# Where sixteen shared-expert steps stand in a fused transformer kernel: all of them in the routing stage, four before the scores of the second half

## The chip, the cores and the metric

The kernel runs on one core of one Trainium2 chip. The metric is the device time of one execution in microseconds (us), as a median of several runs. The engines are named as the profile names them: PE (TensorE, matrix products), DVE (VectorE), ACT (ScalarE), POOL (GpSimd, which here issues the indirect DMAs) and SP (SyncE, which issues plain DMAs).

## The reference, cut to what matters

A sandwich of four sublayers on x of 8 x 256 tokens by 256 channels: each sublayer is `x = x + layernorm(f(layernorm(x)))` with f = attention, a mixture of experts, a state-space layer and a dense feed-forward. The change touches the mixture alone:

```python
logits = flat @ router_w                                   # 2048 x 64
scores = softmax(logits); topk_idx = top_k(logits + router_bias, 4)
# ... the four scores of a token, made to sum to 1, go into comb (2048 x 64)
g = silu(einsum('nd,edf->nef', flat, wg)); u = einsum('nd,edf->nef', flat, wu)
routed = einsum('ne,nef,efd->nd', comb, g * u, wd)         # 64 experts of 64 hidden
sg = silu(einsum('nd,sdh->nsh', flat, swg)); su = einsum('nd,sdh->nsh', flat, swu)
shared = einsum('nsh,shd->nd', sg * su, swd)               # 2 shared experts of 256 hidden
return routed + shared
```

The shared experts have 512 hidden channels in all, and every token passes through them.

## The kernel before

The 2048 tokens are 16 tiles of 128, in four chunks of 512 (NCH = 4, TPC = 4 tiles each). The program is a row of stages, each one block of five instruction streams (one an engine, run in the order written) with a barrier between blocks. Inside a block the streams are ordered by semaphores alone. The stages that matter here are, in order: routing (`stage_route`, L858 to L1288), the routed experts (`stage_slots`, L1291 to L1456), summing (`stage_mid`, L1467 to L1964, which also starts the state-space layer).

**The routing stage** takes the four chunks one after another.
- PE turns the normed rows of a chunk into columns (`turn`, L971, eight transposes of 128 x 128 a chunk) and multiplies them with the router (`score`, L985, 24 products of 64 columns a chunk). ACT and DVE cut each turned bank into a high and a low part (`high_parts` L1073, `low_parts` L1141), because a 32-bit product is made as three products of parts.
- DVE picks the four experts of each token (`choose`, from L1147), PE counts them (`place_chunk`), DVE makes tables of counts (`tables`) and then, for each chunk, the slot of each token and expert (`find_slots`, L1199 to L1220).
- POOL writes the rows to their slots in DRAM by 64 indirect DMAs (`slots_in<-rows,slots`, L957), 16 a chunk, two in flight; before a chunk's first one it waits for that chunk's `find_slots`.
- SP waits for all 64 and then loads the first of 32 groups of slots (`load_quad`, L851), on which the next stage begins.

**A shared-expert step** is one quarter of the hidden channels (SHARED = 4) for one chunk of tokens, so there are sixteen. In a step PE makes gate and up (12 products of 128 x 512: six into `pg`, six into `pu`, L1032), ACT takes silu of the gate (L1111), DVE multiplies (`prod`, L1236), ACT copies the product's high part (`hh`, L1115), DVE subtracts it for the low part (`hl`, L1240), and PE multiplies down (12 products of 256 columns into `acc`, L1042). `pu` is one bank, so the up part of a step waits for the product of the step before. After four steps ACT takes the sum of a chunk out (`take`, `y<-acc`, L1104). The banks `acc0`, `acc1` and `pg0` are also the banks into which `turn` writes.

Eight steps (chunks 0 and 1) stand at the end of the routing stage: on PE behind `place_chunk(3)`, on DVE the first between `find_slots(2)` and `find_slots(3)`, the others behind it, mixed with the work on the tokens' shares (`moved`, `share`, L1282 to L1285). The other eight (chunks 2 and 3) stand at the start of the summing stage. For them the routed-expert stage loads the shared weights again (four loads of 384 KB), and ACT and DVE split them again.

**The summing stage** starts with POOL, which fetches the four expert outputs of every token (`fetch`, `back<-slots_out,slots`, L1582: four indirect DMAs a tile, 64 in all), into eight buffers. DVE adds them into y (`combine`, L1861), and then the chain of two norms of a chunk runs: DVE's statistics, POOL's power (L1590) and shift (L1593), ACT's normed rows (L452), twice, then PE projects the chunk into the state-space layer. POOL's one queue holds the fetches and the two norms of every chunk. Its order is written out:

```python
for i in range(TPC):
    fetch(i)
...
    first = (2, 2, 2, 0)[g]      # tiles of the next chunk fetched ahead of this chunk's norms
    for i in near[:first]: fetch(i)
    deviations(OF_Y, g)
    for i in near[first:first + 1]: fetch(i)
    deviations(OF_X, g)
    for i in near[first + 1:]: fetch(i)
```

Of the kernel before, what the change touches and what calls it, by code (L numbers as in the profile page):

```python
# [5 lines left out]
F32 = mybir.dt.float32  # L6
# [7 lines left out]
P = 128  # L14
# [796 lines left out]
LATE = 2  # L811
NOW = NCH - LATE
LATE_STEPS = SHARED * LATE
# [44 lines left out]
def stage_route(chip, x, rows, norms, xh, xl, y, ident, xs, t, ahead, router, ins):  # L858
# [7 lines left out]
    STEPS = SHARED * NOW  # L866
    slots, share, owner = t["slots"], t["share"], t["owner"]
    wh, wl, bias, sums, places, sh, sl = (router[n] for n in ("wh", "wl", "bias", "sums", "places", "sh", "sl"))
    with ExitStack() as ctx:
# [56 lines left out]
        with nc.Block() as block:  # L926
# [35 lines left out]
            def _(pe):  # L962
# [50 lines left out]

                turn(0)
# [4 lines left out]
                place_chunk(1)  # L1019
                turn(2)  # L1020
                score(2)
                turn(3)
# [4 lines left out]

                def hidden(bank, s, col, c, done):
                    tok = bass.ts(c, CHUNK)
                    terms = [(w, a, k) for k in range(KD) for w, a in ((sh, xh), (sh, xl), (sl, xh))]  # L1030
                    for m, (w, a, k) in enumerate(terms):
                        last = nc.tensor.matmul(bank[:], w[:, s, col + k * P:col + (k + 1) * P], a[:, k, tok],  # L1032
                                                start=(m == 0), stop=(m == len(terms) - 1))
                    last.then_inc(done, 1)

                def down(c, s):
                    pe.wait_ge(lo_done, c * SHARED + (s + 1))
                    if s == 0:
                        after(pe, y_out, c)
                    for i in range(TPC):  # L1040
                        for m, (a, w) in enumerate(((hh, sh), (hh, sl), (hl, sh))):
                            last = nc.tensor.matmul(acc[i // 2][:, i % 2, :], a[:, s % 2, i * P:(i + 1) * P],  # L1042
                                                    w[:, s, 2 * D:3 * D], start=(s == 0 and m == 0 and i % 2 == 0),
                                                    stop=(s == SHARED - 1 and m == 2), skip_group_check=True)
                    last.then_inc(down_done, 1)

                def body(c):
                    first = isinstance(c, int) and c == 0
                    for s in range(SHARED):
                        if not (first and s < 2):  # L1050
                            pe.wait_ge(silu_done, c * SHARED + (s - 1))
                        hidden(pg[s % 2], s, 0, c, gate_done)
                        after(pe, prod_done, c * SHARED + s)
                        hidden(pu, s, D, c, up_done)
                        if s:
                            down(c, s - 1)
                        elif not first:
                            down(c - 1, SHARED - 1)

                repeat(pe, NOW, body)  # L1060
# [3 lines left out]
                down(NOW - 1, SHARED - 1)  # L1064

            @block.scalar
            def _(act):
# [24 lines left out]
                high_parts(0)  # L1092
                high_parts(1)
                scale_y(2)
                scale_y(3)
                fill_rows(2)
                high_parts(2)
                fill_rows(3)
                high_parts(3)

# [6 lines left out]
                for n in range(STEPS):  # L1107
# [8 lines left out]
                    if n == 1:  # L1116
                        act.wait_ge(shifted, 1)
                        nc.scalar.activation(flat(expd[:]), flat(logit[:]), ACT.Exp).then_inc(exp_done, 1)
                    if n % SHARED == 0 and n:
                        take(n // SHARED - 1)  # L1120
                take(NOW - 1)

            @block.vector
            def _(dve):
# [105 lines left out]
                def step(n):  # L1230
# [237 lines left out]
def stage_mid(chip, x, y, xh, xl, ys, moe, t, ident, ins):  # L1468
# [9 lines left out]
    with ExitStack() as ctx:  # L1478
# [67 lines left out]
        with nc.Block() as block:  # L1546
# [70 lines left out]
            def _(pe):  # L1617
# [52 lines left out]
                def late_down(n):  # L1670
                    s = n % SHARED
                    pe.wait_ge(l_lo_done, n + 1)
                    if s == 0 and n:
                        pe.wait_ge(l_out, n // SHARED)
# [1228 lines left out]
```

## Time and profile before

| | |
|---|---|
| median of three runs | 1301.33 us (1296.81 to 1303.6) |
| span of the profiled execution, which is its own time | 1301.3 us, mean granted clock of PE 0.925 |
| routing stage | about 233.8 to 364.1 us |
| routed experts | about 364.1 to 498.4 us |
| summing stage | about 498.4 to 659 us |
| busy share of the span | PE 86%, PE's weight loads 71%, DVE 67%, ACT 47%, POOL 31% |

The stages follow one another with barriers, so a stage costs what its own last chain costs. The table's busy shares are means over stages that differ: in the state-space stages PE is full, in the routing stage it stands idle for long stretches, and in the summing stage POOL is the fullest. The routing stage is read by its end (who ends last there), the summing stage by the start of each chunk's second normed rows.

### The profile page before, as it was taken

Reading aid. Unit: us, or ns where it says so; the run is one execution under the profiler, and the core shown is the slowest. Engines: PE = TensorE matmul, PEld = TensorE weight load, DVE = VectorE, ACT = ScalarE, POOL = GpSimd, SP = SyncE. Lnnn points to the kernel's source line nnn. Section 1 sums busy time; section 2 is a strip of 40 time slices with the busy share of each in tenths; the row PEclk is TensorE's granted clock in tenths of the full one; section 3 lists DMA queues with packets and bytes.
Section 4 is the critical chain, followed back from the end, with each engine's and each line's share of the span. In section 5 each row is a group of like instructions: output and inputs, shape, how many; then the busy total and the mean of one; then the engine's idle time right before and its main releaser. Section 6 shows DMA issues by size and latency. Waiting matters only on the chain. (4 is left out here: it accounts for less than half of the span.)

```text
span 1301.3 us, 31608 instructions
## 1 busy us (share of the span) xinstructions
PE 1123.9 (86%) x12162; PEld 920.4 (71%) x12162; DVE 873.1 (67%) x2172; ACT 615.5 (47%) x1404; POOL 406.1 (31%) x592
## 2 busy tenths in 40 slices
PE   6569998557689997777879999999999999999987
PEld 5446776545478996665647887888788878888776
DVE  6466896757646766688457667667766676664665
ACT  4434456122133443366634554555455545553654
POOL 3331222067700455784038005401530153000221
PEclk9779999557889998888789999999999999999999
DMA  6737884222289884364234334333442332232001
GB/s 171 180 114 203 225 229 169 97 75 87 89 335 414 293 278 160 104 181 148 83 100 120 86 99 131 83 90 100 123 154 86 111 116 85 89 99 85 2 17 49
DMA packets 78562, 177.74 MB, mean 137 GB/s; under 512 B 12678, under 2 KB 26246, under 8 KB 75846
## 3 DMA queue, kind: packets, MB, share of 16 engines
q1 hardware_dynamic: 72140, 158.67, 38.3%
q0 software_dynamic: 6272, 17.05, 4.4%
q8 instruction: 97, 1.59, 0.5%
q14 instruction: 53, 0.43, 0.1%
HBM read 114.40 MB, written 61.08 MB: 135 GB/s over the span
## 5 line engine op out<-in xcount | busy, mean ns | idle before, releaser
L2318 ACT ACTIVATE decay<-masked,negcum 128x128 f32<-128x128 f32 x512 | 163.1, 391 | 101.4 <-DVE mixT L2382 101.4
L2226 PE MATMUL joint<-xh,w_high 128*128 128x512 f32 x512 | 209.2, 409 | 0.0
L2226 PE MATMUL joint<-xl,w_high 128*128 128x512 f32 x512 | 200.1, 391 | 0.0
L2226 PE MATMUL joint<-xh,wl 128*128 128x512 f32 x512 | 199.9, 391 | 0.0
L2430 DVE COPY cT<-joint 128x512 f32<-128x512 f32 x128 | 88.2, 689 | 85.0 <-PE joint L2226 84.8
L2336 ACT ACTIVATE bT<-joint 128x512 f32<-128x512 f32 x128 | 76.6, 599 | 138.1 <-PE joint L2226 138.1
L2382 DVE TENSOR_TENSOR mixT<-pcb,decay 128x512 f32<-128x512 f32 x128 | 82.4, 685 | 60.8 <-PE pcb L2242 60.8
L2159 POOL TENSOR_TENSOR w_high<-w_in,none 128x512 fp32r<-128x512 f32 x32 | 35.4, 1105 | 267.5 <-DMA w_in<-in_w_bc 251.9
L2226 PEld LDWEIGHTS joint<-xh,w_high 128*128 128x128 f32 x512 | 96.2, 188 | 21.2
L2226 PEld LDWEIGHTS joint<-xh,wl 128*128 128x128 f32 x512 | 96.1, 188 | 20.9
L2226 PEld LDWEIGHTS joint<-xl,w_high 128*128 128x128 f32 x512 | 96.3, 188 | 17.0
L2372 DVE TENSOR_TENSOR masked<-cumrow,mask 128x512 f32<-128x512 f32 x128 | 104.8, 819 | 0.1
L697 ACT ACTIVATE probT<-pst 128x384 f32<-128x384 f32 x128 | 60.2, 489 | 64.6 <-PE pst L628 61.1
L2242 PEld LDWEIGHTS pcb<-cT,bT 128*32 128x32 f32 x4096 | 79.4, 110 | 11.7 <-issue 11.7
L2242 PE MATMUL pcb<-cT,bT 128*32 128x128 f32 (+3 forms) x4096 | 84.6, 234 | 0.0
L957 POOL DMA_INDIRECT slots_in<-rows,slots x64 | 66.6, 1041 | 46.1 <-DMA slots_in<-rows,slots 22.5
L1582 POOL DMA_INDIRECT back<-slots_out,slots x64 | 69.6, 1087 | 28.4 <-issue 27.3
L2391 DVE TENSOR_TENSOR cS<-cT,grown 128x256 f32<-128x256 f32 x128 | 61.4, 480 | 12.4 <-ACT grown L2323 1.1
L1448 DVE TENSOR_TENSOR rows<-gate,pgu 64x512 f32<-64x512 f32 x64 | 44.2, 691 | 33.5 <-ACT gate L1423 33.1
L1326 POOL COPY copies<-weights 128x384 f32 x64 | 32.4, 507 | 98.6 <-issue 77.7
L738 DVE CUSTOM_DVE_ANT_0 masked<-ps,reach 128x256 f32<-128x256 f32 x128 | 53.7, 420 | 0.0
L736 DVE CUSTOM_DVE_ANT_0 masked<-ps,reach 128x128 f32<-128x128 f32 x128 | 36.7, 287 | 24.0 <-PE ps L612 23.0
(373 smaller groups left out, 2727.2 us busy)
## 6 DMA issues: line engine op xcount, KB each, us to landing
cumrow<-ssm_cum SPq DMA_DIRECT2D x128, 256.0 KB, 3.3
slots_in<-blank SPq DMA_DIRECT2D x16, 1024.0 KB, 5.3
rows<-slots_in SPq DMA_DIRECT2D x32, 512.0 KB, 5.5
slots_out<-spare SPq DMA_DIRECT2D x32, 512.0 KB, 3.9
weights<-in_expert_quads SPq DMA_DIRECT2D x16, 768.0 KB, 8.7
w_in<-in_w_bc SPq DMA_DIRECT2D x32, 256.0 KB, 3.6
qk_parts<-parts SPq DMA_DIRECT2D x32, 192.0 KB, 2.3
stack<-qk_parts SPq DMA_DIRECT2D x32, 192.0 KB, 5.4
```

What stands on the lines that cost most here:

```text
L697: nc.scalar.activation(probT[:, n % HELD, :], pst[n % T_BANKS][:, 0:3 * P], ACT.Exp).then_inc(exped, 1)
L738: nc.vector.tensor_tensor_reduce(dst[:, P:3 * P], src[:, P:3 * P], reach[:], accum_out=highest[:, u % 2, j, 1:2], **form).then_inc(maxed, 1)
L957: nc.gpsimd.indirect_dma_start(out=xs[:, :], out_offset=bass.IndirectOffsetOnAxis(slots[:, i, k:k + 1], 0), in_=rows[:, i, :], in_offset=N ...
L1582: nc.gpsimd.indirect_dma_start(out=back[:, i % BACK, k, :], out_offset=None, in_=ys[:, :], in_offset=bass.IndirectOffsetOnAxis(slots[:, i, ...
L2226: last = nc.tensor.matmul(bank[:], w[:, j, col:col + P], a[:, k, c * CHUNK:(c + 1) * CHUNK], start=(m == 0), stop=(m == len(parts) - 1))
L2242: last = nc.tensor.matmul(pcb[n % 2][at:at + KEY, reach], bT[:, n % B_BUFS, keys], cT[:, n % 2, reach], start=True, stop=True, skip_group_ ...
L2318: last = nc.scalar.activation(decay[:, n % 2, o], masked[:, n % 2, o], ACT.Exp, bias=negcum[:, c * TPC + i, head:head + 1])
L2336: nc.scalar.activation(bT[:, n % B_BUFS, :], pbT[:], ACT.Copy).then_inc(b_out, 1)
L2372: nc.vector.tensor_tensor(masked[:, n % 2, :].rearrange("p (q l) -> p q l", l=S), cumrow[:, n % CUMS, :].rearrange("p (q l) -> p q l", l=S ...
L2382: nc.vector.tensor_tensor(mixT[:, n % KEEP, :], pcb[n % 2][:], decay[:, n % 2, :], ALU.mult).then_inc(mix_out, 1)
L2391: nc.vector.tensor_tensor(cS[:, n % KEEP, :, :], second, grown[:, n % 2, :, :], ALU.mult).then_inc(c_scaled, 1)
L2430: nc.vector.tensor_copy(cT[:, n % 2, :], pcT[:]).then_inc(c_out, 1)
```

## The change

All sixteen steps stand in the routing stage. Steps 0 to 3 (chunk 0) stand on PE between `place_chunk(1)` and `turn(2)`, and PE waits for ACT's `take(0)` before `turn(2)`, since that writes the banks of the sum; `turn(3)` now stands ahead of `score(2)`. Steps 4 to 15 stand where the eight stood. On ACT the steps 0 and 1 are ahead of `fill_rows(2)`, step 2 ahead of `fill_rows(3)`, step 3 and the take behind it. On DVE the steps 0 and 1 are ahead of `find_slots(1)`, 2 and 3 behind it; in steps 7 to 10 one of the share instructions (`is_equal`) now stands between the product and the low part. The summing stage has no steps, the weights are not loaded and split a second time, and POOL's list `first` starts with 0 in place of 2.

```diff
                 place_chunk(1)
+                pe.wait_ge(logits_out, EARLY_NORMS)
+                for n in range(SHARED):
+                    up(n)
+                    if n:
+                        down(n - 1)
+                down(SHARED - 1)
+                pe.wait_ge(y_out, 1)
                 turn(2)
+                turn(3)
                 score(2)
-                turn(3)
                 score(3)
                 place_chunk(2)
                 place_chunk(3)
                 pe.wait_ge(logits_out, NCH)
-                repeat(pe, NOW, body)
+                for n in range(SHARED, STEPS):
+                    up(n)
+                    if n > SHARED:
+                        down(n - 1)
                 pe.wait_ge(owner_found, 1)
...
-                down(NOW - 1, SHARED - 1)
+                down(STEPS - 1)
...
                 scale_y(3)
+                step(0)
+                step(1)
                 fill_rows(2)
-                high_parts(2)
+                step(2)
                 fill_rows(3)
-                high_parts(3)
+                step(3)
+                take(0)
+                high_parts(2)
+                high_parts(3)
...
                 statistics(x, OF_X, 3)
+                step(0)
+                step(1)
                 find_slots(1)
+                step(2)
+                step(3)
                 low_parts(2)
+                low_parts(3)
                 choose(2)
-                low_parts(3)
                 choose(3)
                 tables(1)
                 find_slots(2)
-                step(0)
+                step(4)
                 find_slots(3)
-                step(1)
+                step(5)
...
-                for n in range(3, STEPS):
+                for k in range(TOPK):
+                    product(7 + k)
+                    link(nc.vector.tensor_tensor(moved[:], place[:],
+                                                 last4[:, :, k:k + 1].broadcast_to([P, NT, NE]), ALU.is_equal))
+                    low(7 + k)
+                    link(nc.vector.tensor_tensor(moved[:], moved[:], expd[:], ALU.mult))
+                    link(nc.vector.tensor_reduce(share[:, :, k], moved[:], AX.X, ALU.add))
+                for n in range(7 + TOPK, STEPS):
                     step(n)
...
-                    if i + DEEP == NQ:
-                        for s in range(SHARED):
-                            sp.dma_start(t["late_raw"][s], ins["shared_w"][:, s, :]).then_inc(t["late_loaded"], 16)
...
-                    first = (2, 2, 2, 0)[g]
+                    first = (0, 2, 2, 0)[g]
...
-                for n in range(LATE_STEPS):
-                    late_step(n)
-                late_down(LATE_STEPS - 1)
```

DVE in the routing stage before, from the last statistics of x to the first low part of chunk 2 (`moved<-ranks` to `slots<-spot` is `find_slots(1)`, `xl` a low part):

```order
L439 TENSOR_SCALAR norm_var<-norm_moments 128x4
L1199 TENSOR_TENSOR moved<-ranks_146,row 128x256
...
L1219 TENSOR_TENSOR spot<-spot 128x16
L1220 TENSOR_TENSOR slots<-spot 128x16
L1141 TENSOR_TENSOR xl<-acc_153,xh 128x2x256
L1141 TENSOR_TENSOR xl<-pg_149,xh 128x2x256
L1147 TENSOR_TENSOR ranked<-pu,router_bias 128x4x64
```

And the same place in the changed kernel:

```order
L439 TENSOR_SCALAR norm_var<-norm_moments 128x4
L1246 TENSOR_TENSOR prod<-gate,pu 128x512
L1252 TENSOR_TENSOR hl<-prod,hh 128x512
L1246 TENSOR_TENSOR prod<-gate,pu 128x512
L1252 TENSOR_TENSOR hl<-prod,hh 128x512
L1209 TENSOR_TENSOR moved<-ranks_145,row 128x256
...
L1230 TENSOR_TENSOR slots<-spot 128x16
L1246 TENSOR_TENSOR prod<-gate,pu 128x512
L1252 TENSOR_TENSOR hl<-prod,hh 128x512
L1246 TENSOR_TENSOR prod<-gate,pu 128x512
L1252 TENSOR_TENSOR hl<-prod,hh 128x512
L1151 TENSOR_TENSOR xl<-acc_152,xh 128x2x256
```

Two steps stand ahead of `find_slots(1)`, two between it and the low parts that the scores of chunk 2 wait for.

DVE at the steps that are mixed with the shares, before:

```order
L1236 TENSOR_TENSOR prod<-gate,pu 128x512
L1240 TENSOR_TENSOR hl<-prod,hh 128x512
L1282 TENSOR_TENSOR moved<-place,last_128 128x1024
L1284 TENSOR_TENSOR moved<-moved,expd 128x1024
L1285 TENSOR_REDUCE share<-moved 128x16
```

And in the changed kernel, where four such groups are followed by five steps with nothing between:

```order
L1246 TENSOR_TENSOR prod<-gate,pu 128x512
L1300 TENSOR_TENSOR moved<-place,last_127 128x1024
L1252 TENSOR_TENSOR hl<-prod,hh 128x512
L1303 TENSOR_TENSOR moved<-moved,expd 128x1024
L1304 TENSOR_REDUCE share<-moved 128x16
```

The first share instruction moved into the place between the product and its low part.

POOL at the start of the summing stage before (a row with x8 is two tiles of the next chunk):

```order
L1582 DMA back<-slots_out,slots 128x256 x16
L1598 MEMSET norm_power 128x4
L1599 MEMSET pad 128x8x3
L1582 DMA back<-slots_out,slots 128x256 x8
L1590 TENSOR_TENSOR norm_rstd<-norm_var,norm_power 128x4
L1593 TENSOR_TENSOR norm_shift<-norm_negmean,norm_rstd 128x4
L1582 DMA back<-slots_out,slots 128x256 x4
```

And in the changed kernel:

```order
L1592 DMA back<-slots_out,slots 128x256 x16
L1608 MEMSET norm_power 128x4
L1609 MEMSET pad 128x8x3
L1600 TENSOR_TENSOR norm_rstd<-norm_var,norm_power 128x4
L1603 TENSOR_TENSOR norm_shift<-norm_negmean,norm_rstd 128x4
L1592 DMA back<-slots_out,slots 128x256 x4
L1600 TENSOR_TENSOR norm_rstd<-norm_var,norm_power 128x4
L1603 TENSOR_TENSOR norm_shift<-norm_negmean,norm_rstd 128x4
L1592 DMA back<-slots_out,slots 128x256 x20
```

The eight fetches of two tiles moved from ahead of chunk 0's first norm to behind its second.

## Rows read from the trace of the kernel before

**Rows 1.** Windows: length, busy PE, PEld, DVE, ACT, POOL, PE clock, DMA share, GB/s.

```profile
233.00:248.00 15.00, 13.40 (x63) 13.03 (x63) 11.46 (x46) 6.42 (x12) 2.41 (x4) 0.50 0.55 211
253.00:272.00 19.00, 0.00 (x0) 0.00 (x0) 16.84 (x74) 0.61 (x2) 8.11 (x9) 0.50 0.12 41
329.00:344.00 15.00, 12.27 (x66) 9.41 (x65) 12.63 (x15) 4.33 (x8) 10.90 (x11) 1.00 0.25 87
```

**Rows 2.** Timeline of POOL, 33rd and last scatter: start, duration, what, idle before.

```profile
310.89 0.96 POOL L957 DMA_INDIRECT slots_in<-rows,slots  x1 [0.82 <-DMA slots_in<-rows,slots]
...
357.57 0.96 POOL L957 DMA_INDIRECT slots_in<-rows,slots  x1 [0.31 <-DMA slots_in<-rows,slots]
```

**Rows 3.** Timeline of PE in the routing stage and at the next stage's start.

```profile
272.53 1.12 PE L971 MATMUL acc<-ident,rows 128*128 128x128 f32 x4 [20.06 <-ACT rows L452]
...
275.15 0.39 PE L985 MATMUL pu<-router_wh,xh 128*128 128x64 f32 x1 [0.52 <-DVE xl L1141]
...
284.03 0.39 PE L985 MATMUL pg<-router_wh,xh 128*128 128x64 f32 x1 [1.80 <-DVE xl L1141]
...
303.07 0.52 PE L1032 MATMUL pu<-xh,router_sh 128*128 128x512 f32 x1 [4.02 <-DVE prod L1236]
...
305.52 0.41 PE L1042 MATMUL acc<-router_sh,hh 128*128 128x256 f32 x1
...
327.81 0.40 PE L1032 MATMUL pg<-xh,router_sh 128*128 128x512 f32 x1
...
328.98 0.40 PE L1032 MATMUL pg<-xh,router_sl 128*128 128x512 f32 x1
...
364.11 3.84 PE L1359 MATMUL pt<-ident,rows 128*128 128x128 f32 x16 [12.70 <-PEq L926]
```

**Rows 4.** Timeline of DVE in the routing stage.

```profile
266.91 0.42 DVE L1199 TENSOR_TENSOR moved<-ranks,row 128x256 f32<-128x256 f32 x1
...
289.37 0.42 DVE L1147 TENSOR_TENSOR ranked<-pg,router_bias 128x256 f32<-128x256 f32 x1 [4.89 <-PE pg L985]
...
302.33 0.68 DVE L1236 TENSOR_TENSOR prod<-gate,pu 128x512 f32<-128x512 f32 x1
...
308.68 0.68 DVE L1236 TENSOR_TENSOR prod<-gate,pu 128x512 f32<-128x512 f32 x1
...
323.29 0.69 DVE L1236 TENSOR_TENSOR prod<-gate,pu 128x512 f32<-128x512 f32 x1
324.68 0.69 DVE L1240 TENSOR_TENSOR hl<-prod,hh 128x512 fp32r<-128x512 f32 x1 [0.70 <-ACT hh L1115]
...
329.06 0.69 DVE L1236 TENSOR_TENSOR prod<-gate,pu 128x512 f32<-128x512 f32 x1
```

**Rows 5.** Timeline of ACT: the last take of the routing stage.

```profile
351.45 1.09 ACT L1104 ACTIVATE y<-acc 128x512 f32<-128x512 f32 x2 [3.74 <-PE acc L1042]
```

**Rows 6.** Timeline of POOL in the summing stage.

```profile
502.83 1.42 POOL L1582 DMA_INDIRECT back<-slots_out,slots  x1 [0.30 <-issue]
...
522.02 0.95 POOL L1582 DMA_INDIRECT back<-slots_out,slots  x1 [0.30 <-issue]
...
533.97 1.17 POOL L1590 TENSOR_TENSOR norm_rstd<-norm_var,norm_power 128x4 f32<-128x4 f32 x1
```

**Rows 7.** Timeline of DVE in the summing stage.

```profile
524.89 3.25 DVE L1861 SCALAR_TENSOR_TENSOR y<-back,share,y 128x256 f32<-128x256 f32 x8 [0.88 <-DMA back<-slots_out,slots]
...
530.17 1.40 DVE L1890 BATCH_NORM_STATS2 norm_stats<-y 128x6 f32<-128x256 f32 x4
```

**Rows 8.** Timeline of ACT in the summing stage: the second normed rows of chunks 0 to 3.

```profile
542.89 2.08 ACT L452 ACTIVATE y<-x,norm_shift,norm_rstd 128x256 f32<-128x256 f32 x4 [2.38 <-POOL norm_shift L1593]
...
568.42 2.08 ACT L452 ACTIVATE y<-x,norm_shift,norm_rstd 128x256 f32<-128x256 f32 x4 [2.64 <-POOL norm_shift L1593]
...
593.21 2.08 ACT L452 ACTIVATE y<-x,norm_shift,norm_rstd 128x256 f32<-128x256 f32 x4 [1.88 <-POOL norm_shift L1593]
...
618.03 2.08 ACT L452 ACTIVATE y<-x,norm_shift,norm_rstd 128x256 f32<-128x256 f32 x4 [0.77 <-POOL norm_shift L1593]
```

More of the change, by code:

```diff
@@ L1012, in place_chunk, with hidden, up, down @@
                     rank(g)
+                def hidden(bank, s, col, c, done):
+                    tok = slice(c * CHUNK, (c + 1) * CHUNK)
+                    terms = [(w, a, k) for k in range(KD) for w, a in ((sh, xh), (sh, xl), (sl, xh))]
+                    for m, (w, a, k) in enumerate(terms):
+                        last = nc.tensor.matmul(bank[:], w[:, s, col + k * P:col + (k + 1) * P], a[:, k, tok],
+                                                start=(m == 0), stop=(m == len(terms) - 1))
+                    last.then_inc(done, 1)
+                def up(n):
+                    c, s = n // SHARED, n % SHARED
+                    if n >= 2:
+                        pe.wait_ge(silu_done, n - 1)
+                    hidden(pg[n % 2], s, 0, c, gate_done)
+                    if n:
+                        pe.wait_ge(prod_done, n)
+                    hidden(pu, s, D, c, up_done)
+                def down(n):
+                    c, s = n // SHARED, n % SHARED
+                    pe.wait_ge(lo_done, n + 1)
+                    if s == 0 and c:
+                        pe.wait_ge(y_out, c)
+                    for i in range(TPC):
+                        for m, (a, w) in enumerate(((hh, sh), (hh, sl), (hl, sh))):
+                            last = nc.tensor.matmul(acc[i // 2][:, i % 2, :], a[:, n % 2, i * P:(i + 1) * P],
+                                                    w[:, s, 2 * D:3 * D], start=(s == 0 and m == 0 and i % 2 == 0),
+                                                    stop=(s == SHARED - 1 and m == 2), skip_group_check=True)
+                    last.then_inc(down_done, 1)
                 turn(0)
@@ L1026, in _ @@
                 pe.wait_ge(logits_out, NCH)
[L1028 to L1048, printed above, removed]
-                    for s in range(SHARED):
[L1050 to L1058, printed above, removed]
-                repeat(pe, NOW, body)
+                for n in range(SHARED, STEPS):
+                    up(n)
+                    if n > SHARED:
+                        down(n - 1)
                 pe.wait_ge(owner_found, 1)
@@ L1105, in take, with step @@
                     last.then_inc(y_out, 1)
-                for n in range(STEPS):
+                def step(n):
                     act.wait_ge(gate_done, n + 1)
@@ L1241, in step @@
                                             ALU.subtract).then_inc(lo_done, 1)
+                def step(n):
+                    product(n)
+                    low(n)
                 statistics(y, OF_Y, 2)
@@ L1476, in stage_mid @@
     val = t["val"].rearrange("p v (t n) -> p v t n", n=P)
-    sh, sl, l_gate, prod, hh, hl = (t["late"][n] for n in ("sh", "sl", "gate", "prod", "hh", "hl"))
     with ExitStack() as ctx:
@@ L1918, in convolve @@
                             n += 1
-                for s in range(SHARED):
-                    split(s)
                 dve.wait_ge(raw_loaded, 16)
```

139 lines of the change are left out of this document (18 added, 121 removed).

## The prediction

> **What bounds the kernel now.** I read four views: windows over the routing stage for where PE is idle, the timelines of POOL and ACT at its end for who ends last, the timelines of PE and DVE for what a step costs, and the timelines of POOL and ACT in the summing stage for what its chunks wait for.
>
> PE does nothing from 253 to 272, 19 us long, and DVE is busy 16.84 of them [rows 1]. That is where the change puts four steps: PE has the room, DVE has 2 us. In the tail of the steps, 329 to 344, DVE is busy 12.63 of 15 and PE 12.27. The routing stage is ended by POOL: the last scatter starts at 357.57 [rows 2], SP's load waits for it, and PE's first transposes of slots start at 364.11 after 12.70 idle [rows 3]. The last step's take starts at 351.45 and lasts 1.09 [rows 5], so the steps end at 352.54, 11.6 ahead. The scatters take (357.57 - 310.89) / 31 = 1.51 each. In the summing stage, a chunk's second normed rows on ACT wait for POOL in all four chunks [rows 8], and POOL is full of fetches: from the sixteenth's start at 522.02 to the first norm at 533.97 it runs nine, 1.33 each, with no idle [rows 6].
>
> **The early steps, by which the scores are late.** In what follows a time is on the clock of the profile before.
> - Step 0's product starts on DVE where `find_slots(1)` started, 266.91, and ends at 267.6 [rows 4]. Then PE makes the up part of step 1, for which `pu` had to come free: after 4.02 idle six products took 2.45 [303.07 to 305.52, rows 3], so 270.1, and with the hand-over product 1 starts at 270.4.
> - From a product's start to its low part's end it is 324.68 + 0.69 - 323.29 = 2.08: 272.5. `find_slots` is what is left of 302.33 to 308.68 beside a step, 6.35 - 2.08 = 4.27 [rows 4]: 276.8. Its chunk's scatters come after sixteen of chunk 0, at about 310.89 - 16 x 1.51 = 286.7, so this delay is hidden by 10 us.
> - Step 2's product ends at 277.5. On ACT its high part (0.70, DVE's wait for one at 324.68) is followed by `fill_rows(3)`, 2.08 as the same line takes in [rows 8], and only then by silu of step 3, which I price like the high part: product 3 at 281.0, low part done at 283.1.
> - PE's down: twelve products of 256 columns. Gate products run at (328.98 - 327.81) / 5 = 0.234 in the fast stretch, half of it is 0.117: 1.4, so 284.5. ACT's take is 1.09 [rows 5]: 285.6. Now `turn(2)` may write the banks.
> - Before, `turn(2)` to the first score was 275.15 - 272.53 = 2.6 [rows 3]. Now `turn(3)` stands between, with two waits for halves; four transposes take 1.0 to 1.1, and I add 1.4 for what doesn't lie beside other work: 289.6.
> - Two scores: one from 284.03 to DVE's use at 289.37 is 5.34, the other 5.1: 300.05. `choose(3)` started at 289.37 before: **10.7 late**.
>
> Everything behind `choose(3)` on DVE is the same until the tail, so it is 10.7 late too. That includes `find_slots(2)`, which ended at 302.33: 313.0, against 310.89 for the first scatter that needs it. POOL loses 2.4, and its chain alone would let PE start at 366.5. It is no longer the last.
>
> **The tail.** Step 7 is the old step 3: product at 323.29 + 10.7 = 334.0. A step with share work took 329.06 - 323.29 = 5.77, of which 0.70 is DVE's wait for the high part [rows 4]; `is_equal` now fills it, so four steps at 5.07: product 11 at 354.3. Behind it nothing is mixed in, and PE sets the pace: the up half of step 12 (six, 1.4) ends at 356.5; then each step is 12 x 0.234 + 1.4 = 4.2, three of them 369.1; the last step's product and low part 371.4, down 372.8, take 374.1. With 0.4 for the barrier PE begins the slots at 374.5 in place of 364.11: **+10.4**. By then the first groups have lain in the buffers for 8 us. Before, the sixteen first transposes stretched over 3.84 [rows 3]. Between nothing and 3.8 for that head start I take 1.3, since later groups are bound by PE. **+9.1** net. The routed-expert stage loses four loads; it is bound by PE, so I give nothing.
>
> **The summing stage.** PE's eight late steps go, but they stood beside POOL's fetches. A fetch beside the splitting of weights took 1.42 against 0.95 later [rows 6]; for two such I let the first sixteen end 0.9 earlier, at 522.1. The last two tiles' sum on DVE started 524.89, 3.25 long, behind the landing [rows 7]: now 524.0 to 527.3, statistics 1.40 and their ends 0.7: 529.4. Before, POOL fetched two tiles meanwhile; now its queue holds the norm of chunk 0 there and it **idles 7.3 us**. Chunk 0's second rows start earlier: norm 530.5, four fetches 5.3, second norm: 537.6 in place of 542.89. But up to chunk 1's second rows POOL's queue holds the same 44 fetches and four norms in both orders; with 7.3 of idle, less the 0.9, and less 1.0 that it waited before (542.89 - 533.97 is 8.9, two norms of 1.3 and four fetches are 7.9), they come up to 5.4 later than 568.42. By 1.33 a fetch they come at 572.0, 3.6 later. I take 4. Chunk 2's rows carry that, and chunk 3's give back about 1, since their wait for POOL was only 0.77 of ACT's idle [rows 8]: **+3.0** at the end of the stage.
>
> **The sum.** The profiled execution is 1301.3, the median 1301.33, so no correction: 1301.3 + 9.1 + 3.0 = 1313.4. I say 1313. 0.5%, about what a measurement of this kernel can tell from no change, is 6.5 us: 1294.8 to 1307.8.
>
> **A rule against this sum.** From 233 to 248 the granted clock was 0.50, 1.2 GHz, though PE was busy 13.40 of 15 with transposes and scores [rows 1]; steps in the tail ran at 1.00, 2.4 GHz. So I price both scores at the lower clock, 10.4. The Trainium skill, "TensorE: Matmul & The Clock Gate", "Part 1: The HAM clock gate", says that the throttled state is the default and that activity releases it. By it the four steps ahead of the scores could hand them the full clock; the 233 to 248 row does not agree for scores that come with no steps ahead of them, and no row shows scores behind steps.
>
> **The rivals.**
> - *The scores get the full clock.* The steps end at 284.5 and the scores start 5 us later, with transposes between. For it: steps run at 1.00. Against it: scores at 0.50, and a wait of 4.02 after which products were slow again. If it holds, scores take half, 5.2 less, transposes 1.0 less: 1313.4 - 6.2 = 1307.2, inside 0.5%: not slower. It decides from 5.6 us saved. I give it 0.18, with half savings among it.
> - *Fetches get faster* without steps beside them: 0.95 and 0.30 of issue is 1.25 [rows 6]. 44 fetches at 1.25 and not 1.33 are 3.5 less, the summing stage comes out even: 1310. For it: the shortest rows. Against: DVE and ACT now work on norms beside them. 0.17.
> - *The early steps are slower than I price*, since PE is at 1.2 GHz through up 2, up 3 and down 3 (twice 2.8 more than at the full clock and 1.4, of which 4 show, since DVE's own work covers the rest), and the summing stage costs 1.5 more, as its bound of 5.4 says: 1313.4 + 4 + 1.5 = 1318.9. 0.12.
> - *The tail is hidden after all*, with the first slot groups giving back all of 3.8 and chunk 0's head start in the summing stage kept, so that its rows go 5.3 earlier through all chunks: 1301.3 + 10.4 - 3.8 - 5.3 = 1302.6. Against: rows 8, where each chunk waits for POOL. 0.05; only with a mistake of mine elsewhere would it be faster, 0.03.
> - The forecast itself, 1311 to 1316, has 0.45.
>
> The range from 1305 to 1319 leaves out the last cases of both ends, under 2 in 10. Of the chances, the clock's and the fetches' lower ends and the hidden tail make 0.20 within 0.5%, faster 0.04, slower 0.76.
>
> **What would show it.** DVE's `ranked<-pg` of the last score about 300 and `find_slots(2)` done about 313 show the early steps; the 33rd scatter at 313 to 314 shows that POOL lost little; ACT's last `y<-acc` behind SP's first slot load, at 373, shows that the steps took the stage's end over; PE's granted clock over 289 to 300 decides the first rival. In the summing stage an idle of about 7 us on POOL ahead of its first norm, chunk 0's second rows 5 earlier and chunk 1's 4 later after the shift of stages show the second term. I am wrong if the scores run at 2.4 GHz, if DVE's 2.08 a step shrinks because nothing waits, or if POOL's fetches speed up.

## The result and the profile after

The changed kernel takes 1308.69 us (median of 7 runs, 1303.42 to 1311.74), the kernel before 1301.31 beside it (7 runs, 1296.81 to 1305.24). The ratio is 1.0061, 95% interval [1.0037, 1.0086]: 0.6% slower, 7.4 us by the medians, where 12 were forecast. The profiled execution of the changed kernel has a span of 1309.9, 8.6 over the one before. A span is some 1.8 shorter than the time of its execution; this one's time, 1311.74, is the highest of the seven.

Where the 8.6 went can be read at four marks: PE's first transposes of the routing stage, its first transposes of slots, POOL's first fetch of the summing stage, and chunk 3's second normed rows. The routing stage is 5.3 longer (232.13 to 367.74, against 233.80 to 364.11), the routed experts 1.2 shorter (134.55 against 135.72), the summing stage up to chunk 3's rows 5.8 longer (123.99 against 118.20). The part ahead of these marks came out 1.7 shorter and the part behind them 0.4 longer; the change touches neither.

Windows over the routing stage of the changed kernel, columns as in [rows 1]:

```profile
233.00:248.00 15.00, 14.21 (x70) 13.35 (x69) 11.05 (x47) 7.72 (x13) 2.42 (x4) 0.50 0.53 211
253.00:272.00 19.00, 9.44 (x37) 7.73 (x36) 14.87 (x56) 3.99 (x8) 9.48 (x11) 0.71 0.12 42
272.00:289.00 17.00, 13.40 (x93) 11.86 (x91) 8.45 (x23) 7.93 (x15) 12.05 (x13) 1.00 0.27 93
289.00:300.00 11.00, 9.74 (x55) 8.10 (x55) 7.82 (x43) 0.02 (x1) 7.14 (x8) 0.60 0.28 98
329.00:344.00 15.00, 14.37 (x74) 10.67 (x73) 14.69 (x16) 4.41 (x9) 11.81 (x10) 1.00 0.24 81
```

PE's idle stretch holds 9.44 of work now. The next two windows are the news: from 272 to 289 the granted clock is 1.00, 2.4 GHz, and it is still up when the scores begin. The first window, scores with no steps ahead, is at 0.50 as before. From 329 to 344 DVE is full, 14.69 of 15, where it had 2.4 to spare.

Timeline of PE from the last down product of the early steps to the scores, and at the start of the slots:

```profile
232.13 1.94 PE L968 MATMUL acc<-ident,rows 128*128 128x128 f32 x8 [1.05 <-PEq L521]
...
282.86 0.28 PE L1035 MATMUL acc<-router_sh,hl 128*128 128x256 f32 x1
284.31 0.66 PE L968 MATMUL acc<-ident,rows 128*128 128x128 f32 x4 [1.18 <-ACT y L1098]
...
286.86 0.28 PE L982 MATMUL pu<-router_wh,xh 128*128 128x64 f32 x1
...
289.54 0.28 PE L982 MATMUL pg<-router_wh,xh 128*128 128x64 f32 x1
...
291.10 0.38 PE L982 MATMUL pg<-router_wh,xl 128*128 128x64 f32 x1
291.30 0.40 PE L982 MATMUL pg<-router_wh,xh 128*128 128x64 f32 x1
...
367.74 1.06 PE L1377 MATMUL pt<-ident,rows 128*128 128x128 f32 x8 [1.43 <-PEq L923]
```

And PE in the kernel before, at the transposes that followed the first of the two scores:

```profile
280.26 1.97 PE L971 MATMUL acc<-ident,rows 128*128 128x128 f32 x8
```

The first score takes 289.54 - 286.86 = 2.68, where it took 5.11 before (from 275.15 [rows 3] to 280.26). In the second the single products go from 0.28 to 0.40 at 291.10: the clock falls there.

Timelines of DVE, ACT, POOL and SP of the changed kernel, in that order: the last score's use, products 7, 11 and 15, the first and last takes, the last scatter, the first load of slots.

```profile
293.44 0.42 DVE L1157 TENSOR_TENSOR ranked<-pg,router_bias 128x256 f32<-128x256 f32 x1 [0.91 <-PE pg L982]
...
327.39 0.69 DVE L1246 TENSOR_TENSOR prod<-gate,pu 128x512 f32<-128x512 f32 x1
...
347.29 0.69 DVE L1246 TENSOR_TENSOR prod<-gate,pu 128x512 f32<-128x512 f32 x1
...
362.47 0.69 DVE L1246 TENSOR_TENSOR prod<-gate,pu 128x512 f32<-128x512 f32 x1 [2.14 <-PE pu L1015]
...
283.17 1.09 ACT L1098 ACTIVATE y<-acc 128x512 f32<-128x512 f32 x2 [2.51 <-PE acc L1035]
...
366.34 1.09 ACT L1098 ACTIVATE y<-acc 128x512 f32<-128x512 f32 x2 [2.51 <-PE acc L1035]
...
355.71 1.23 POOL L954 DMA_INDIRECT slots_in<-rows,slots  x1 [0.30 <-DMA slots_in<-rows,slots]
...
359.73 9.42 SPq L848 DMA_DIRECT2D rows<-slots_in  x4
```

The last take ends at 367.43, 7.7 behind SP's first load, and PE's slots begin 0.3 later: the steps end the routing stage now. Product 7 to product 11 takes 19.90, four steps of 4.98; the last product waits 2.14 for PE.

Timeline of POOL and ACT in the summing stage of the changed kernel (the ACT rows answer to [rows 8]):

```profile
502.29 1.02 POOL L1592 DMA_INDIRECT back<-slots_out,slots  x1 [10.76 <-issue]
...
533.24 1.05 POOL L1600 TENSOR_TENSOR norm_rstd<-norm_var,norm_power 128x4 f32<-128x4 f32 x1 [7.01 <-DVE norm_var L439]
...
540.98 2.08 ACT L452 ACTIVATE y<-x,norm_shift,norm_rstd 128x256 f32<-128x256 f32 x4 [42.90 <-POOL norm_shift L1603]
...
575.76 2.08 ACT L452 ACTIVATE y<-x,norm_shift,norm_rstd 128x256 f32<-128x256 f32 x4 [4.85 <-POOL norm_shift L1603]
...
601.62 2.08 ACT L452 ACTIVATE y<-x,norm_shift,norm_rstd 128x256 f32<-128x256 f32 x4 [2.54 <-POOL norm_shift L1603]
...
626.28 2.08 ACT L452 ACTIVATE y<-x,norm_shift,norm_rstd 128x256 f32<-128x256 f32 x4 [0.68 <-POOL norm_shift L1603]
```

POOL stands idle 7.01 ahead of its first norm. Counted from the first fetch (502.29; 499.83 in the trace of before), the second rows of the four chunks start 4.4 earlier, 4.9 later, 6.0 later and 5.8 later than before.

### The profile page after: what moved, and what is told of

Same layout as the page of the kernel before. It is cut to its first block and busy times, and to the rows that moved or that the text cites. A ratio compares the mean times of both kernels' runs of the same rounds, so it can differ in the third digit from the quotient of the medians.

```text
span 1309.9 us, 31598 instructions
## 1 busy us (share of the span) xinstructions
PE 1119.1 (85%) x12162; PEld 914.8 (70%) x12162; DVE 872.2 (67%) x2168; ACT 614.6 (47%) x1400; POOL 410.6 (31%) x592
## 5 line engine op out<-in xcount | busy, mean ns | idle before, releaser
L954 POOL DMA_INDIRECT slots_in<-rows,slots x64 | 68.8, 1074 | 43.7 <-DMA slots_in<-rows,slots 19.2
L1592 POOL DMA_INDIRECT back<-slots_out,slots x64 | 69.4, 1085 | 29.1 <-issue 28.5
L1634 PE MATMUL turned<-ident,y 128*128 128x128 f32 x32 | 8.3, 433 | 58.2 <-ACT y L452 58.2
```

Source lines behind the costliest of these rows:

```text
L954: nc.gpsimd.indirect_dma_start(out=xs[:, :], out_offset=bass.IndirectOffsetOnAxis(slots[:, i, k:k + 1], 0), in_=rows[:, i, :], in_offset=N ...
L1592: nc.gpsimd.indirect_dma_start(out=back[:, i % BACK, k, :], out_offset=None, in_=ys[:, :], in_offset=bass.IndirectOffsetOnAxis(slots[:, i, ...
```

## The experiments

All ratios are to the kernel before, run on the same chip. The three lengths are read from each run's one profiled execution, between the marks named above.

| run | ratio [95%] | routing | routed experts | summing, to chunk 3's rows |
|---|---|---|---|---|
| before | 1 | 130.3 | 135.7 | 118.2 |
| changed | 1.0061 [1.0037, 1.0086] | 135.6 | 134.6 | 124.0 |
| a_first2 | 1.0012 [0.9998, 1.0026] | 137.4 | 133.5 | 117.1 |
| a_first1 | 1.0032 [1.0019, 1.0046] | 134.8 | 134.5 | 116.4 |
| b_first0 | 1.0068 [1.0043, 1.0093] | 128.7 | 137.3 | 127.8 |
| a_first111 | 1.0063 [1.0040, 1.0087] | 134.0 | 133.4 | 121.7 |
| a_share_back | 1.0084 [1.0054, 1.0115] | 138.7 | 135.1 | 121.7 |
| a_flight4 | 1.0059 [1.0038, 1.0079] | 135.6 | 133.7 | 121.3 |
| b_flight4 | 0.9937 [0.9915, 0.9959] | 120.4 | 135.8 | 118.5 |
| b_fill | 0.9977 [0.9955, 0.9998] | 130.0 | 135.4 | 116.1 |
| b_fill79 | 0.9983 [0.9968, 0.9998] | 125.6 | 135.5 | 118.5 |
| early4_late8 | 0.9992 [0.9972, 1.0013] | 126.1 | 136.5 | 116.7 |
| late4_if4 | 0.9960 [0.9941, 0.9979] | 124.4 | 137.0 | 117.1 |

A length repeats to a few us only. Where two scatters are in flight and the scatters end the stage, the routing stage came out between 125.6 and 130.3. Much of that goes with the clock of the first half's scores, which stand ahead of every step: none of their 48 products ran at the pace of 2.4 GHz where the stage took 128.7 to 130.3 (before, b_first0, b_fill), 18 and 15 where it took 125.6 and 126.1 (b_fill79, early4_late8). The summing stage with the changed list (changed, a_share_back, a_flight4) came out between 121.3 and 124.0. So 5.8 for the summing stage is the high end: the mean of those three, 122.3, is 4.7 over the mean of before, b_flight4, b_fill, b_fill79 and early4_late8 (117.6), which have the old list and the eight late steps.

**POOL's list in the summing stage.** First the old list in the changed kernel (a_first2), then one tile ahead (a_first1), then the new list in the kernel before (b_first0):

```diff
-                    first = (0, 2, 2, 0)[g]
+                    first = (2, 2, 2, 0)[g]
```

> The changed kernel with POOL's old list (2, 2, 2, 0) in the summing stage. Theory M1 (the 7 us in which POOL stands idle ahead of chunk 0's first norm make the whole stage late): no idle, chunk 3's second rows start 118 us after the stage's first fetch as in the kernel before (124.0 in the changed kernel), the time falls by 5.8 to about 1303. Rival M2 (the stage is later because of something else that came with the removal of the late steps, such as fetches that take longer): 124 stays, 1308 to 1309.

> The changed kernel with the list (1, 2, 2, 0): one tile fetched in the idle stretch, which is about as long as four fetches (5.3 us). M1: chunk 0's second rows stay as early as in the changed kernel, chunk 1's come 5.3 earlier, the time falls by 5 to 6, to about 1303, like with the old list. M2: 1308 to 1309.

> The kernel before with the new list (0, 2, 2, 0). M1: POOL stands idle from 523 until DVE's statistics behind the late steps, at about 532, and chunk 3's second rows come 6 to 9 later: 1307 to 1310. M2 (the order costs nothing by itself): 1301.

Timeline of POOL in a_first2, the last fetch ahead of chunk 0's first norm, and that norm:

```profile
536.26 0.95 POOL L1592 DMA_INDIRECT back<-slots_out,slots  x1 [0.30 <-issue]
537.23 1.05 POOL L1600 TENSOR_TENSOR norm_rstd<-norm_var,norm_power 128x4 f32<-128x4 f32 x1
```

And the same norm in b_first0, with chunk 3's second rows on ACT (the first fetch started at 496.02):

```profile
529.64 1.05 POOL L1590 TENSOR_TENSOR norm_rstd<-norm_var,norm_power 128x4 f32<-128x4 f32 x1 [9.01 <-DVE norm_var L439]
...
623.86 2.08 ACT L452 ACTIVATE y<-x,norm_shift,norm_rstd 128x256 f32<-128x256 f32 x4 [2.12 <-POOL norm_shift L1593]
```

With the old list the idle is gone, chunk 3's rows come 117.1 after the first fetch, and the loss shrinks from 0.6% to 0.1% (0.3% at most, by its interval). In the kernel before the new list makes 9.01 of idle, chunk 3's rows come 9.6 later and the time goes up by 0.7%. M1 holds from both sides, and M2 falls. One tile ahead (a_first1) leaves 1.79 of idle, and its summing stage is as short as with the old list; its ratio is a little higher than a_first2's, but the two intervals overlap. By the medians a_first2 leaves 2.8 of the 7.4 us lost and a_first1 3.5 (1300.89 and 1301.61, the kernel before beside them 1298.10), so the list cost 4 to 5.

**Fewer fetches ahead of the later chunks.**

```diff
-                    first = (0, 2, 2, 0)[g]
+                    first = (1, 1, 1, 0)[g]
```

> The changed kernel with the list (1, 1, 1, 0): of the next chunk one tile is fetched ahead of each chunk's first norm and one ahead of its second. Theory M1 (POOL's queue sets chunk 1's and chunk 2's second rows): 40 fetches in place of 44 stand ahead of chunk 1's, which come 5 earlier than with (1, 2, 2, 0), 63 us after the first fetch in place of 67.9; chunk 3's come up to 5 earlier too, 111 to 116 in place of 116.4: 1297 to 1302. Rival M3 (PE's and ACT's pace of 24 a chunk is the bound by then): chunk 1's rows earlier, chunk 3's not, time as with (1, 2, 2, 0).

Timelines of a_first111: POOL at chunk 2's first norm, and ACT's second rows of chunks 1 to 3 (the first fetch started at 498.46).

```profile
582.25 1.47 POOL L1600 TENSOR_TENSOR norm_rstd<-norm_var,norm_power 128x4 f32<-128x4 f32 x1 [2.91 <-DVE norm_var L439]
```

```profile
563.45 2.08 ACT L452 ACTIVATE y<-x,norm_shift,norm_rstd 128x256 f32<-128x256 f32 x4 [3.55 <-POOL norm_shift L1603]
...
591.91 2.08 ACT L452 ACTIVATE y<-x,norm_shift,norm_rstd 128x256 f32<-128x256 f32 x4 [3.77 <-POOL norm_shift L1603]
...
620.16 2.08 ACT L452 ACTIVATE y<-x,norm_shift,norm_rstd 128x256 f32<-128x256 f32 x4 [3.67 <-POOL norm_shift L1603]
```

Neither expectation came true. Chunk 1's rows come 65.0 after the first fetch, 2.9 ahead of a_first1's, but then it is 28.5 and 28.3 to the next chunk, not 24 to 25. The queue holds the same sixteen fetches and two norms a chunk, and now an idle as well (2.91 here, 1.79 ahead of the first norms of chunks 0 and 1). Two tiles between a chunk's last fetch and its first norm cover DVE's sum and statistics, as a_first2 shows; one doesn't.

**The tail of the steps.**

```diff
                     product(7 + k)
-                    link(nc.vector.tensor_tensor(moved[:], place[:], ..., ALU.is_equal))
                     low(7 + k)
+                    link(nc.vector.tensor_tensor(moved[:], place[:], ..., ALU.is_equal))
```

> The changed kernel with the share instructions behind both halves of a step again (product, low part, compare, multiply, sum). Theory R1 (DVE sets the pace of steps 7 to 10 and nothing behind them has slack): product 7 to product 11 takes 23.1 in place of 19.9 (four waits of 0.70 come back), PE begins the slots 2.8 to 3.2 later, the time is 3 more than the changed kernel's, about 1.008 of the kernel before. Rival R2 (something else ends the stage): no difference.

Timeline of DVE in a_share_back, product 7 and product 11:

```profile
326.78 0.69 DVE L1246 TENSOR_TENSOR prod<-gate,pu 128x512 f32<-128x512 f32 x1
...
349.84 0.69 DVE L1246 TENSOR_TENSOR prod<-gate,pu 128x512 f32<-128x512 f32 x1
```

23.06 in place of 19.90, and PE begins the slots 3.1 later. From DVE's use of the last score to PE's first transposes of slots it is 77.6 here, and 74.0 to 74.5 in the five other traces with this routing stage: what DVE loses in the tail, the stage loses. R1 holds by the trace; the ratio moved the same way, but its interval overlaps that of the changed kernel.

**Four scatters in flight**, in the changed kernel and in the kernel before:

```diff
-IN_FLIGHT = 2
+IN_FLIGHT = 4
```

> The changed kernel with four scatters in flight in place of two. Theory R1 (in the changed kernel the steps end the routing stage, PE waits for the last take alone): the last scatter and SP's first load come some 8 to 10 earlier, and PE begins the slots as late as in the changed kernel, 135.6 us after the first transposes of the stage: nothing is won, 1.0061 against the kernel before. Rival R2 (the scatters and loads still hold the start of the slots): 5 to 8 less, as in the kernel before with four in flight (0.9937).

> The kernel before with four scatters in flight in place of two. Theory S1 (in the kernel before the routing stage is ended by the chain of scatters, and each pair waits for its landing): a scatter takes 1.26 to 1.3 (0.96 and 0.30 of issue) in place of 1.51, the last one starts some 13 earlier, the stage is then ended by the steps, PE begins the slots at about 355 in place of 364.1, and the time falls by about 9 to 1292. Rival S2 (the writes themselves need 1.5 each): nothing changes, 1301.

Timelines of POOL, ACT, SP and PE in b_flight4: the last scatter, the last take, the first load of slots, the slots' first transposes.

```profile
345.95 0.96 POOL L957 DMA_INDIRECT slots_in<-rows,slots  x1 [0.30 <-issue]
...
347.41 1.08 ACT L1104 ACTIVATE y<-acc 128x512 f32<-128x512 f32 x2 [3.75 <-PE acc L1042]
...
348.44 6.33 SPq L851 DMA_DIRECT2D rows<-slots_in  x4
...
352.49 3.84 PE L1359 MATMUL pt<-ident,rows 128*128 128x128 f32 x16 [5.12 <-PEq L926]
```

Timelines of SP, ACT and PE in a_flight4, and the group of its scatters (busy time, mean ns, idle before by releaser):

```profile
355.37 14.44 SPq L848 DMA_DIRECT2D rows<-slots_in  x4
...
367.00 1.08 ACT L1098 ACTIVATE y<-acc 128x512 f32<-128x512 f32 x2 [2.51 <-PE acc L1035]
...
368.40 1.06 PE L1377 MATMUL pt<-ident,rows 128*128 128x128 f32 x8 [1.43 <-PEq L923]
...
L954 POOL DMA_INDIRECT slots_in<-rows,slots x64 | 68.6, 1072 | 40.0 <-DVE slots L1230 21.3 <-issue 17.8 <-DMA slots_in<-rows,slots 0.9
```

The same edit takes 0.6% from the kernel before and nothing from the changed one, whose routing stage is 135.6 long with two and with four: R1 holds, and S1 in the main. From first to last the scatters of the kernel before took 87.4 in place of 95.6. A scatter took 1.40 from the 33rd on (345.95 - 302.66, over 31), less than 1.51 but more than the 1.26 to 1.3 expected, and the scatters still end that stage: PE begins 4.05 behind SP's first load, as before (360.06 to 364.11), and the last take ended 4.0 ahead. In the changed kernel the last scatter came only 3.5 earlier against the first (91.9 against 95.4), not 8 to 10; part of the reason stands in the last row: POOL waited 21.3 in all for slots, of which 18.8 is the wait ahead of the first scatter, so 2.5 for slots that DVE found late.

**The clock at the scores.** Products that nobody reads in PE's idle stretch of the kernel before, 68 and then 79 of them:

```diff
                 place_chunk(1)
+                pe.wait_ge(logits_out, EARLY_NORMS)
+                for m in range(68):
+                    nc.tensor.matmul(pu[:], sh[:, 0, 0:P], xh[:, 0, 0:CHUNK], start=(m == 0), stop=(m == 67))
                 turn(2)
```

> The kernel before with 68 products of 128 x 512 into a bank that nobody reads, on PE in its idle stretch between the places of chunk 1 and the columns of chunk 2; nothing else is changed. Theory C1 (the scores of the second half run at the full clock in the changed kernel because PE was at work until shortly before): the first of the two scores takes about 2.7 in place of 5.1, the second between 2.7 and 5.1, and from the first transposes of chunk 2 to DVE's use of the last score it is 11 to 14 in place of 16.8; the total stays, 1298 to 1301, since the scatters end the stage. Rival C2 (the other order of columns and scores made them shorter): 16.8 stays.

> The kernel before with 79 products of 128 x 512 in PE's idle stretch in place of 68: they last until about 271.4, so that PE stands idle under 1 us, and not 2.79, before the transposes of chunk 2. Theory C1, narrowed (the scores keep the full clock if PE is at work until shortly before; 2.79 of idle was too long, 1.79 and 1.18 in the changed kernel were not): 11 to 14 from those transposes to DVE's use of the last score. Rival C2 (not the clock handed on by earlier products, but the order of columns and scores): 16.8 as with 68. The total stays at 1298 to 1301 by both.

Windows over b_fill, then over b_fill79, then over a_first2 (its scores of the second half); columns as in [rows 1]:

```profile
253.00:272.00 19.00, 16.21 (x67) 12.74 (x67) 16.01 (x69) 1.54 (x4) 8.81 (x11) 0.95 0.12 42
272.00:289.00 17.00, 14.68 (x70) 13.41 (x69) 5.80 (x21) 6.17 (x11) 12.01 (x13) 0.50 0.27 93
```

```profile
253.00:268.00 15.00, 15.00 (x66) 12.03 (x64) 13.14 (x56) 0.82 (x2) 8.32 (x9) 1.00 0.16 54
268.00:272.00 4.00, 3.03 (x23) 2.26 (x21) 1.38 (x2) 3.73 (x9) 3.00 (x5) 1.00 0.19 66
```

```profile
281.00:286.00 5.00, 3.98 (x19) 3.81 (x20) 1.88 (x3) 3.00 (x6) 2.99 (x4) 0.50 0.23 80
286.00:296.00 10.00, 10.00 (x51) 9.99 (x52) 3.74 (x18) 0.36 (x1) 7.38 (x8) 0.50 0.30 105
```

Timeline of PE in b_fill79, at the transposes and in the first score:

```profile
268.32 0.65 PE L971 MATMUL acc<-ident,rows 128*128 128x128 f32 x4
...
270.61 0.27 PE L985 MATMUL pu<-router_wh,xh 128*128 128x64 f32 x1 [0.64 <-DVE xl L1144]
...
271.94 0.35 PE L985 MATMUL pu<-router_wh,xh 128*128 128x64 f32 x1
272.10 0.40 PE L985 MATMUL pu<-router_wl,xh 128*128 128x64 f32 x1
```

And DVE's use of the last score in a_first2:

```profile
295.84 0.42 DVE L1157 TENSOR_TENSOR ranked<-pg,router_bias 128x256 f32<-128x256 f32 x1 [2.33 <-PE pg L982]
```

With 68 products PE stood idle 2.79 ahead of the transposes, and the scores ran at 0.50 throughout: from the transposes to the last score's use it was 16.8, as without any. Theory C1 failed in the form in which it was stated. With 79 products, which reach up to the transposes, the transposes and half of the first score ran at 1.00, and the clock fell at 271.94: 15.2 in place of 16.8. So earlier work can hand the full clock on, which the order alone (C2) doesn't explain, but less than expected here.

The other traces say how far this goes. Of the 48 products of the second half's scores, none ran at the pace of 2.4 GHz in the three traces in which PE had stood idle for about 20 us ahead of the transposes (before, b_first0, b_flight4). Of the eight traces with steps there, six have 36 to 40 (the changed kernel 38), a_first1 has 21, and a_first2 has none, though these two differ from the changed kernel in POOL's list alone, which comes later. In a_first2 PE stood idle 2.11 ahead of the last down product and 1.18 ahead of the transposes, the clock fell within that down product (its products go from 0.28 to 0.41 at 280.22), and the two scores took 10.46 (285.38 to 295.84), which is the length that the forecast gave them. In a_first1 these idles were 1.14 and 1.18. So the idle alone isn't shown to decide: b_fill's 2.79 and a_first2's 2.11 stood ahead of a fallen clock and the changed kernel's 1.79 ahead of a full one, but a_first1, with the shortest, kept it for fewer products. Each of these is one execution.

Neither filling moved the total by more than 0.3%; the scatters end that kernel's routing stage.

**One part of the change alone**: the routing code of the changed kernel cut to eight steps (0 to 3 early, 4 to 7 at the end), with the summing stage of before.

```diff
-    STEPS = SHARED * NCH
+    STEPS = SHARED * NOW
...
```

> One part of the change alone: steps 0 to 3 stand early as in the changed kernel, steps 4 to 7 at the end of the routing stage, and the other eight stay in the summing stage of the kernel before, with its weights and its list (2, 2, 2, 0). Theory R1 (early steps make the scores late by about 5, which the scatters don't notice): the last scatter 0 to 2 later against the stage's start, the steps end well ahead of it, 1.000 against the kernel before, within 0.3%. Rival R3 (what is late at the scores is late at the stage's end): 4 to 5 us more, 1.0035.

Timelines of DVE and PE in early4_late8 (the stage's first transposes were at 232.83):

```profile
292.41 0.42 DVE L1160 TENSOR_TENSOR ranked<-pg,router_bias 128x256 f32<-128x256 f32 x1 [1.07 <-PE pg L985]
...
358.94 1.30 PE L1385 MATMUL pt<-ident,rows 128*128 128x128 f32 x5 [28.11 <-PEq L926]
```

The last score's use is 4.0 later than before against the stage's start (59.6, 55.6), PE stands idle 28.11 ahead of the slots, and the time is that of before, 0.9992. Early steps are free as long as the scatters end the stage: R1 holds, R3 falls.

**Four late steps and four scatters in flight**: early4_late8 with three chunks in the routing stage, one in the summing stage, and the edit of b_flight4.

```diff
-LATE = 2
+LATE = 1
...
-IN_FLIGHT = 2
+IN_FLIGHT = 4
...
```

> A version that should beat both: twelve steps in the routing stage (four early, eight at the end), the four of chunk 3 in the summing stage, the list (2, 2, 2, 0), and four scatters in flight. If the steps end the routing stage (R1), PE begins the slots about 120 us after the stage's first transposes, as in the kernel before with four in flight (120.4), and the summing stage has four steps less: 0.991 to 0.994 of the kernel before. If four steps in the summing stage give POOL or DVE a new wait, 0.995 to 1.000.

The group of scatters in late4_if4:

```profile
L957 POOL DMA_INDIRECT slots_in<-rows,slots x64 | 68.5, 1071 | 38.4 <-DVE slots L1233 19.6 <-issue 17.8 <-DMA slots_in<-rows,slots 0.9
```

0.9960, faster than both kernels, but not better than b_flight4 (0.9937), as was hoped. The summing stage, 117.1, shows no new wait. The steps ended at 350.57; PE began the slots at 355.84, 124.4 after the stage's first transposes and 4.04 behind SP's first load, so the scatters ended the stage. Of POOL's 19.6 of waiting for slots 17.13 lay ahead of the first scatter; 2.5 was for slots found late, which was nothing to the kernel with two in flight and is something with four. b_flight4 has the lowest ratio of all versions that were run, though its interval overlaps that of late4_if4.

## Why the prediction was right, point by point

The time fell into the range and on the side that was forecast; the change came out at 7.4 and not at 12, with one step too dear and one too cheap. That it was slower by more than 0.5% is in part luck. 1308.69 lies outside the 1311 to 1316 of the forecast itself and nearer to the first rival's 1307.2, and by its own words ("I am wrong if the scores run at 2.4 GHz") the prediction failed in one step. The two errors partly cancel: with the summing stage at the forecast's 3.0 instead of 4.7 to 5.8 the time would have been 1306 to 1307 by estimate, in the range but within the 0.5%. The shares don't fit, either: 9.1 of 12.1 were forecast for routing and routed experts, which cost 4.1 of 8.6 in the profiled execution, and 2.8 (a_first2) or 3.5 (a_first1) of 7.4 by the medians of the kernels without most of the idle.

- **The early steps up to the take: right.** The take was forecast to end, and so to free the banks, at 285.6; it ended at 284.26 in a trace whose routing stage began 1.67 earlier, 285.9 on the clock of before.
- **"So I price both scores at the lower clock, 10.4": the step that failed.** Transposes to first score took 2.55 where 4.0 was forecast, and the two scores 6.6 (286.86 to 293.44) where 10.4 was. So `choose(3)` was 5.7 late and not 10.7. The first rival's mechanism, given 0.18, is what happened: 5.0 of its 6.2 was saved, since the clock fell in the second score. That the saving reached the end is shown by the five traces with this tail: from the last score's use to the slots they took 74.0 to 74.5, with scores at 2.4 GHz as well as, in a_first2, at 1.2. In a_first2 the two scores took what was forecast, 10.46, so this step failed in the changed kernel and in most traces of its code, but not in every one. The Trainium skill, "TensorE: Matmul & The Clock Gate", "Part 1: The HAM clock gate", has activity release the throttle. The trace of the changed kernel agrees with it by 1.00 over 272 to 289 behind steps and 0.50 over 233 to 248 without them; that of a_first2, with 0.50 over 286 to 296 behind the same steps and PE busy 10.00 of 10, doesn't.
- **The tail and the stage's new end: right.** Steps 7 to 10 took 19.90, forecast 20.3; the three steps in which PE sets the pace took 12.67 (349.80 to 362.47), forecast 12.6; the take ended the stage, and four scatters in flight changed nothing. POOL lost nothing: its 33rd scatter started at 308.67, 310.3 on the clock of before, not 313.
- **+9.1 for routing and routed experts: measured 4.1 in the profiled execution** (5.3 less 1.2), which is 9.1 less the clock's 5.0. So close a fit is chance: by the means of the five traces with this routing stage (269.4 for the two stages; a_share_back left out) and of the two with the unchanged old one (before, b_first0: 266.0) it is 3.4. The give-back of 1.3 was nearly the measured 1.2; the mean of the routed experts is 134.1 in the six traces with twelve steps at the tail and 136.0 in the six with eight late steps, so it may be 1.9, and what it comes from isn't shown.
- **+3.0 for the summing stage: the term that was too small.** The idle was forecast at 7.3 and is 7.01. Chunk 1's rows were to be 4 later and are 4.9. What failed is "chunk 3's give back about 1". POOL's last fetch came 6.0 later against the first (103.60, before 97.65), and behind it chunk 3's first norm waited 9.77 for DVE's statistics, 9.94 before: there was nothing to give back, and the loss stayed, 5.8 in this execution and 4.7 in the mean of three. Also, the first sixteen fetches won none of the 0.9: the sixteenth started 22.69 behind the first, before 22.19. a_first2 and b_first0 show that the idle is the cause.
- **The rival of faster fetches** (0.17) came true in part. From the sixteenth fetch's end to chunk 1's second rows POOL has 28 fetches and four norms in both kernels; without the idle that took 42.8, before 44.5 (less its wait of 0.94). So 1.7 of the 3.5 was won there in these two executions, and 0.9 by the means of the three traces with the changed list (42.9) and the five with the old one and eight late steps (43.8). That didn't decide: a_first2, with the old list and no late steps, has 117.1 where the kernels with the old list and eight late steps have 117.6 in the mean.

What is not settled is what decides whether the scores keep the clock of the steps. It fell after 38 score products in the changed kernel, after about 12 in b_fill79, and ahead of the transposes in a_first2, and no run here tells why.

## What to carry to other kernels

Before moving work into an idle stretch, look at what ends the stage and how far behind the moved work's own end is: eight steps ended 11.6 ahead of the slots' first transposes and were free, and twelve at the tail were not, however idle PE was elsewhere. In a queue that is full until its last waiter is served, idle comes back at the end: 7.01 and 9.01 of idle on POOL cost the summing stage 4.7 to 5.8 and 9.6, while 1.79 (a_first1) cost nothing that the trace shows. Work that stands ahead of a wait and fills it is worth the idle that it prevents, so count it before you move it away. The cheapest gain lay in neither place but in the chain that ended the stage, where four scatters in flight in place of two took 0.6% from the kernel before.

## What the runs showed of the hardware that was not expected

- The full clock was handed over a gap, but not always: after steps at 1.00 and PE idle for 1.79 and 1.18, the transposes and 38 of 48 score products of the changed kernel still ran at 2.4 GHz (0.111 from one to the next, against 0.213). In a_first2, with the same work on PE, all 48 ran at 1.2 GHz.
- From 286 to 296 in a_first2 the granted clock was 0.50 while PE was busy 10.00 of 10, almost all of it with score products.
- Scores without steps ahead of them differ between executions, too: the first half's 48 products all ran at the lower clock in six of the thirteen traces, the changed kernel's among them, and 13 to 24 of them ran at the full one in the other seven.
- Two indirect scatters in flight left POOL waiting for landings: 22.5 us in all before (19.2 in the changed kernel). With four the same wait was 0.9 in both kernels, and a scatter's mean busy time was unchanged (1.041 and 1.042 in the kernel before). Of the 21.6 saved there 13.4 came back as time of issue (4.7, then 18.1), so the chain got 8.1 shorter.
